# One gather DMA for each sequence by reordered LoRA rows, and the sums of h stored by the sync queue

## The chip, the cores and the metric

The kernel runs on one core of a Trainium2 chip. Its time is what the device takes for one execution, in microseconds (us); lower is better.

## The reference

`x` has 64 sequences of 64 tokens and 512 features, and each sequence has an adapter number from 0 to 7. The first part is a gated MLP with LoRA adapters, the second a matrix of 64x64 for each sequence, chosen by the same number:

```
gate = x @ Wg + (x @ Ag[i]) @ Bg[i]          # 512 -> 2048, rank 16
up   = x @ Wu + (x @ Au[i]) @ Bu[i]
h    = silu(gate) * up
x    = x + h @ Wd + (h @ Ad[i]) @ Bd[i]      # 2048 -> 512
x    = x + einsum('bct,bcd->bdt', x, W1[i])  # mixes the 64 tokens of a sequence
```

## The kernel before

**Tiling.** The first phase (gate, up and h) has 64 steps: 4 groups of 16 sequences (1024 tokens), and in each group 16 chunks of 128 columns of the hidden size. A step makes its chunk of gate and up for a group with seven products of half size in place of eight (a Strassen-like scheme: sums of the quarters of x and of the weights). Every product is made of three matmuls on a high and a low part of each operand (lines 1368 to 1370), for each half of the 256 rows it sums over. The second phase (h times Wd, then the 64x64 mix) goes over 16 blocks of four sequences, again with seven products each (lines 1517 to 1519). It reads h, and the sums and differences of h that its products need, back from `h_dram`.

**The LoRA rows.** The x @ A result of a group is in `t_st`. For each pair of steps (a piece of two chunks, `PIECE = 2`; 32 pieces in all) the tile `bq[n % 2]` holds the rows of B for the 16 sequences of the group, in 4 quads of 4 sequences: for each sequence 16 ranks, and these twice, once for the high and once for the low part of t. That makes 4 sequences x 16 ranks x 2 = 128 partitions. Partition of a row: `half * 64 + sequence * 16 + rank`. Line 1380 multiplies with `bq` and takes 256 columns; its four uses in a step have 4 matmuls each, and the one for `l22_done` comes first, behind the products A11 and S1.

**Gathers.** Which rows of `b_dram` go into `bq` depends on the adapter number, which SP reads into a register (`number`). `gather_b` issues for each sequence two DMAs, one for each half, each of 16 rows of 4 KB (64 KB). A piece takes 32 DMAs, 16 in each of two loop turns of SP. Piece `n` may be issued when piece `n - 2` has been used (`p4_done`), since `bq` has two buffers. The first piece goes another way: `gather_raw` fetches rows of `b_gu` into `bq_raw`, and ACT and POOL split them.

**Queues.** Each engine works in the written order. SP's turn `s` of 1 to 63 loads the weights for step `s + 2` (`load_w`, line 236), stores h of step `s - 1` when it is made (`store_even` or `store_odd`, line 245), gathers half of piece `s // 2 + 1` (line 276), and once in a group loads x of the next (line 241). The sums of h (`hs1` to `hs3`, made by DVE at lines 1001, 1007, 1013 and 1019) are stored by POOL at line 473, whose other work in a step is little: `gather_a` (line 447) copies the A columns of each sequence into `aq`, and a few steps split B for `b_dram`. DVE waits for a store to have landed (`h_stored`) before it writes the same tile again, in `make_s4` even for the store of `hs2` of the step before. Behind the last turn SP issues `load_n4` (line 284), which fills `wd_raw_n4` for the second phase.

Of the kernel before, what the change touches and what calls it, by code (L numbers as in the profile page):

```python
# [11 lines left out]
P = 128  # L12
# [14 lines left out]
PIECE = 2  # L27
PIECES = CH // PIECE
BC = 2 * WB
GATHER = SLOTS * 2 * 16  # L30


PAIRS, KC = 16, CH // 2
# [25 lines left out]
def cond_resid_kernel(nc, x, xg, idx, packed, wd, a_gu, b_gu, a_d, b_d, w1, slot_mask, tok_mask, eye, out):  # L59
    ctx = ExitStack()  # L60
    with ctx:
# [6 lines left out]
        def at(name, offset, shape, dt=F32):  # L68
            return nc.alloc_sbuf_tensor_at(name, shape, dt, offset=base + offset)
# [14 lines left out]
        bq = [at(f"bq{i}", 147456 + i * 16384, [P, QUADS, PIECE, BC], F32R) for i in range(2)]  # L84
        t_st = [[at(f"t_st{u}{i}", 180224 + i * 8192 + u * KIB4, [P, GT], F32R) for i in range(2)] for u in range(2)]
        a_all = at("a_all", 196608, [P, ADAPTERS, KT * 2, RANK])
        aq = [at("aq", 200704, [P, KT * 2, QS, RANK])] + [at(f"aq{q}", 202752 + q * 2048, [P, KT * 2, QS, RANK])
                                                        for q in range(1, QUADS)]
        bq_raw = at("bq_raw", 139264, [P, QUADS, PIECE, WB])
        t_f = at("t_f", 202752, [P, QT])  # L90
# [123 lines left out]
        def piece_of(g, k):  # L214
            return PIECES - 1 - k if g % 2 else k
# [14 lines left out]
        def _(sp):  # L230
# [21 lines left out]
            def store_odd(s):  # L252
# [2 lines left out]
                sp.wait_ge(h1_done, s + 1)  # L255
                store_op(s, H12, h_f[1], 0)

            slot_numbers = {}

            def gather_raw(b):  # L260
                slot_numbers[b] = number(sp, b)
                for half in range(2):
                    r = half * QR + (b % QS) * RANK
                    sp.dma_start(bq_raw[r:r + RANK, b // QS, :, :],
                                 b_gu[0, bass.ds(slot_numbers[b], 1)].rearrange("a r k c -> (a r) k c"))\
                        .then_inc(bq_raw_in[2 * b // SLOTS], 16)

            def gather_b(n, first, last):
                g, k = divmod(n, PIECES)
                sp.wait_ge(b_stored, 16 * (k if g == 0 else PIECES))  # L270
                if n >= 2:
                    sp.wait_ge(p4_done, 2 * n - 2)
                for b in range(first, last):
                    for half in range(2):
                        r = half * QR + (b % QS) * RANK
                        sp.dma_start(bq[n % 2][r:r + RANK, b // QS, :, :].bitcast(F32).rearrange("r k c -> r (k c)"),  # L276
                                     b_dram[piece_of(g, k), bass.ds(slot_numbers[g * SLOTS + b], 1)].rearrange("a r c -> (a r) c"))\
                            .then_inc(bq_in[n % 4], 16)

            def load_parts(op, a, source):  # L280
                k = 0
# [68 lines left out]
            def load_ad(p):  # L350
                if p == 0:
                    sp.wait_ge(p4_done, STEPS - 2)
                else:
                    sp.wait_ge(ad_lo_done, 4 * p)
                for b in range(QS):
                    a = number(sp, seq_of(p, b))
                    sp.dma_start(ad_raw[:, b, :, :, :].rearrange("p e k r -> p (e k r)"),
                                 a_d[bass.ds(a, 1)].rearrange("a p c -> (a p) c")).then_inc(ad_in, 16)
# [24 lines left out]
            for s in range(1, STEPS):  # L383
                if fresh(s + 2):
                    load_w(s + 2)
                if s % 2:
                    store_even(s - 1)
                else:
                    store_odd(s - 1)
                if s >= 2 and s // 2 + 1 < GROUPS * PIECES:  # L390
                    at = s % 2 * (SLOTS // 2)
                    gather_b(s // 2 + 1, at, at + SLOTS // 2)
                if 5 <= s % CH < 13 and s // CH + 1 < GROUPS:
                    for b in range(2 * (s % CH - 5), 2 * (s % CH - 4)):
                        b += (s // CH + 1) * SLOTS
                        slot_numbers[b] = number(sp, b)
                if s % CH == 2 and s // CH + 1 < GROUPS:
                    load_x(s // CH + 1)
                if s == STEPS - CH + 1:
                    load_wd11()  # L400
                    load_wd12()
                if s == STEPS - CH + 2:
                    load_wd22_early()
                if s == STEPS - CH + 3:
                    load_wd21_early()
                if s == STEPS - CH + 7:
                    store_t3()
                if s == STEPS - CH + 11:
                    store_n4()
                if s == STEPS - 2:  # L410
                    load_h(0)
                    load_ad(0)
# [13 lines left out]
            for n in range(3, PAIRS * PRODUCTS):  # L426
                p, i = divmod(n, PRODUCTS)
                if n + 4 < PAIRS * PRODUCTS:
                    load_h(n + 4)
                if i == 3 and p + 1 < PAIRS:  # L430
                    load_bd(p + 1)
                if i == 5 and p + 2 < PAIRS:
                    load_ad(p + 2)
            p = PAIRS - 1
            for j in (1, 0):
                sp.wait_ge(y_done[j], p + 1)
# [4 lines left out]
        def _(pool):  # L441
            def gather_a(g, q):
                if g:
                    pool.wait_ge(t_done, g * QUADS + q)
                for s in range(QS):
                    a = number(pool, g * SLOTS + q * QS + s)
                    pool.tensor_copy(aq[q if g == 0 else 0][:, :, s, :], a_all[:, bass.ds(a, 1), :, :].rearrange("p a k r -> p (a k) r"))\
                        .then_inc(a_gathered, 1)

            def load_b(i):  # L450
# [14 lines left out]
            def bq0_lo(pair):  # L465
# [1 line left out]
                pool.wait_ge(bq0_hi_done, pair + 1)  # L467
                pool.tensor_tensor(bq[0][:, q, :, WB:2 * WB], bq_raw[:, q, :, :], bq[0][:, q, :, 0:WB].bitcast(F32),
                                   ALU.subtract).then_inc(bq0_lo_done, 1)

            def store_sum(s, op, tile, col):
                g, k = s // CH, chunk_of(s) // 2
                pool.dma_start(h_dram[PPG * g:PPG * (g + 1), op, :, k, :].rearrange("q p t -> p q t"),  # L473
                               tile[:, col:col + HALF].rearrange("p (q t) -> p q t", q=PPG)).then_inc(h_stored[op], 16)

            def store_s3(n):
                pool.wait_ge(hs3_done, n + 1)
                store_sum(2 * n, HS3, hs3, 0)

            def store_s12(n):  # L480
                pool.wait_ge(hs1_done, n + 1)
                store_sum(2 * n, HS1, hs1, 0)
                pool.wait_ge(hs2_done, n + 1)
                store_sum(2 * n, HS2, hs2, 0)

            def store_s4(n):
                pool.wait_ge(hs4_done, n + 1)
                store_sum(2 * n, HS4, hs2, 0)

            def load_tables():  # L490
                pool.wait_ge(p4_done, 2 * CH)
# [65 lines left out]
            for s in range(1, STEPS):  # L557
                g, c = divmod(s, CH)
                late = LATE_T if g == 0 else 0
                if s < PIECES:  # L560
                    b_lo(s)
                    store_b(s)
                    if s + 1 < PIECES:
                        load_b(s + 1)
                if g + 1 < GROUPS and 4 <= c - late < 8:
                    gather_a(g + 1, c - late - 4)
                if s == 2 * CH:
                    load_tables()
                if s == 2 * CH + 3:
                    store_tables()  # L570
                if s % 2:
                    store_s3(s // 2)
                    if s >= 3:
                        store_s4(s // 2 - 1)
                else:
                    store_s12(s // 2 - 1)
            load_res(0)
            make_zeros()
            load_mix(0)
            store_s12(STEPS // 2 - 1)  # L580
            load_res(1)
            store_s4(STEPS // 2 - 1)
            for p in range(1, PAIRS):
                load_mix(p)
                if p + 1 < PAIRS:
# [6 lines left out]
        def _(act):  # L592
# [40 lines left out]

            def bq0_hi(pair):
                q = slice(2 * pair, 2 * pair + 2)
                act.wait_ge(bq_raw_in[pair], 16 * SLOTS)
                hi(bq[0][:, q, :, 0:WB], bq_raw[:, q, :, :]).then_inc(bq0_hi_done, 1)

            def t_hi(g, q):
# [721 lines left out]
        def _(pe):  # L1361
# [23 lines left out]
            def lora_a(g, q):  # L1385
                i = g * QUADS + q
                pe.wait_ge(a_gathered, QS * (i + 1))
                if q == 0:
                    for k in range(4):
                        pe.wait_ge(x_in[k], 16 * (g + 1))  # L1390
                bank = T_BANKS[q] if g == 0 else RT
                if g:
                    pe.wait_ge(t_masked, i if q else 1)
                a = aq[q if g == 0 else 0]
                n = slice((q % 2) * QT, (q % 2 + 1) * QT)
                for k in range(KT):
                    src = xst[(B11, B12, B21, B22)[2 * (k // 2) + q // 2]][:, (k % 2) * HALF:(k % 2 + 1) * HALF]
                    m = pe.matmul(bank[:, 0:QT], a[:, k * 2:k * 2 + 2, :, :].rearrange("p u s r -> p (u s r)"),  # L1398
                                  src[:, n], start=k == 0, stop=k == KT - 1)
                m.then_inc(t_done, 1)  # L1400

# [240 lines left out]
```

## Time and profile before

| | |
|---|---|
| median of 3 runs | 1218.6 us (1215.49 to 1220.42) |
| the profiled execution: its time | 1219.65 us |
| its span, first to last instruction | 1218.0 us |
| mean granted TensorE clock | 0.982 of full speed |
| busy: PE, DVE, ACT, POOL | 1163.6, 913.6, 539.3, 256.3 us |
| DMA over the span | 276.26 MB, mean 227 GB/s |

The busy time of PE is modelled from its pipelined matmuls; what it waited for is read from the table of waits. A name like `bq<-b_dram` is a tile and what it was filled from, buffer numbers left out. `SPq` is the sync engine's queue of instructions.

### The profile page before, as it was taken

What the parts mean: (1) busy time and instruction counts of PE and PEld (TensorE: products, weight loads), DVE (VectorE), ACT (ScalarE), POOL (GpSimd) and SP (SyncE); (2) the same over time, 40 slices, a digit from 0 to 9 for tenths busy, and PEclk for the clock granted to TensorE, in tenths of its full rate; (3) what the DMA queues carried; (4) which work ended last, traced back from release to release, by engine and by line L of the source; (5) the groups of instructions that cost most, each with busy time, mean ns of one, the idle gap of its engine ahead of it and who ended that gap; (6) DMA issues with size and microseconds to landing.
All of it is one profiled execution on the core that took longest, in us unless ns stands there. A gap on an engine that the chain in (4) does not pass through costs nothing.

```text
span 1218.0 us, 23035 instructions
## 1 busy us (share of the span) xinstructions
PE 1163.6 (96%) x6720; PEld 1034.8 (85%) x6720; DVE 913.6 (75%) x1578; ACT 539.3 (44%) x902; POOL 256.3 (21%) x405
## 2 busy tenths in 40 slices
PE   4889999999999997999999999998899999999998
PEld 3678888887888886888888788887899999999997
DVE  6776777876787787678887788888667766776775
ACT  4544444543444443344453344456344444444442
POOL 5223221112201012220101111011322221231230
PEclk8899999999999999899999999999999999999999
DMA  5597876688667589666759978868777777667781
GB/s 188 161 308 241 244 222 180 170 235 262 189 180 234 171 238 264 190 194 187 233 166 274 280 223 252 243 215 307 244 265 244 244 239 273 232 230 274 231 277 66
DMA packets 155583, 276.26 MB, mean 227 GB/s; under 512 B 28898, under 2 KB 97634, under 8 KB 155330
## 3 DMA queue, kind: packets, MB, share of 16 engines
q1 hardware_dynamic: 133104, 213.48, 57.5%
q0 software_dynamic: 21488, 59.66, 14.6%
q10 hardware_dynamic: 866, 1.66, 0.4%
q8 instruction: 54, 0.88, 0.3%
q14 instruction: 71, 0.58, 0.2%
HBM read 200.23 MB, written 74.45 MB: 226 GB/s over the span
## 4 chain that ended last, share of the span: by engine, by line
PE 73%; SPq 9%; DVE 5%; DMA 5%; issue 4%; ACT 3%; POOL 1%; POOLq 0%; DVEq 0%; ACTq 0%
PE ps L1368 12%; PE ps L1369 12%; PE ps L1370 12%; PE ps L1517 8%; PE ps L1519 8%; PE ps L1518 8%; PE ps L1380 7%; SPq L276 7%; DMA bq<-b_dram 2%; PE ps L1398 2%; DMA h_raw<-h_dram 1%; DMA xst<-xg 1%; SPq L245 1%; ACT xo_hi L602 1%; SPq L199 1%
## 5 line engine op out<-in xcount | busy, mean ns | idle before, releaser
L1368 PE MATMUL ps<-xo_hi,w_hi 128*128 128x512 f32 x896 | 359.3, 401 | 12.0 <-DVE w_lo L886 10.7
L1369 PE MATMUL ps<-xo_lo,w_hi 128*128 128x512 f32 x896 | 354.8, 396 | 0.0
L1370 PE MATMUL ps<-xo_hi,w_lo 128*128 128x512 f32 x896 | 351.8, 393 | 0.0
L1368 PEld LDWEIGHTS ps<-xo_hi,w_hi 128*128 128x128 f32 x896 | 171.4, 191 | 43.0 <-DVE w_lo L886 10.7
L1370 PEld LDWEIGHTS ps<-xo_hi,w_lo 128*128 128x128 f32 x896 | 170.4, 190 | 38.2
L473 POOL DMA_DIRECT2D h_dram<-hs x128 | 96.0, 754 | 487.3 <-DVE hs L1001 247.9
L886 DVE TENSOR_TENSOR hl<-h_raw,hh 128x1024 fp32r<-128x1024 f32 x112 | 137.0, 1223 | 79.0 <-ACT hh L602 77.6
L1380 PEld LDWEIGHTS ps<-t_st,bq 128*128 128x128 f32 x1024 | 158.5, 193 | 44.2 <-DMA bq<-b_dram 18.0
L1369 PEld LDWEIGHTS ps<-xo_lo,w_hi 128*128 128x128 f32 x896 | 171.1, 191 | 26.6
L1380 PE MATMUL ps<-t_st,bq 128*128 128x256 f32 x1024 | 166.2, 286 | 21.7 <-DMA bq<-b_dram 15.9
L602 ACT ACTIVATE hh<-h_raw 128x1024 fp32r<-128x1024 f32 x112 | 117.9, 1053 | 113.3 <-DMA h_raw<-h_dram 72.0
L886 DVE TENSOR_TENSOR w_lo<-wsum,w_hi 128x512 fp32r<-128x512 f32 x116 | 83.1, 717 | 60.2 <-ACT w_hi L602 60.2
L674 ACT ACTIVATE u_s<-u_s 128x512 f32<-128x512 f32 x64 | 40.5, 633 | 145.6 <-DVE u_s L973 145.6
L1517 PE MATMUL ps<-wd_t,hh 128*128 128x256 f32 x256 | 73.2, 286 | 5.5 <-DVE hl L886 3.8
L1517 PE MATMUL ps<-wd,hh 128*128 128x288 f32 x256 | 76.6, 299 | 0.0
L986 DVE TENSOR_TENSOR h_f<-u_s,v 128x512 f32<-128x512 f32 x64 | 44.2, 690 | 41.7 <-ACT u_s L674 41.7
L1518 PE MATMUL ps<-wd,hh 128*128 128x288 f32 x256 | 75.4, 295 | 0.0
L670 ACT ACTIVATE p_s<-p_s 128x512 f32<-128x512 f32 x64 | 40.5, 633 | 78.5 <-DVE p_s L956 78.4
L1519 PE MATMUL ps<-wd,hl 128*128 128x288 f32 x256 | 75.2, 294 | 0.0
L602 ACT ACTIVATE w_hi<-wsum 128x512 fp32r<-128x512 f32 x116 | 72.2, 623 | 5.4 <-DVE wsum L919 5.4
L1518 PE MATMUL ps<-wd_t,hh 128*128 128x256 f32 x256 | 72.9, 285 | 0.0
L1519 PE MATMUL ps<-wd_t,hl 128*128 128x256 f32 x256 | 72.9, 285 | 0.0
(153 smaller groups left out, 2188.0 us busy)
## 6 DMA issues: line engine op xcount, KB each, us to landing
bq<-b_dram SPq DMA_DIRECT2D x992, 64.0 KB, 2.6
h_raw<-h_dram SPq DMA_DIRECT2D x112, 512.0 KB, 5.3
h_dram<-hs POOLq DMA_DIRECT2D x128, 256.0 KB, 4.2
raw<-packed SPq DMA_DIRECT2D x58, 512.0 KB, 4.0
h_dram<-h_f SPq DMA_DIRECT2D x96, 256.0 KB, 3.9
ad_raw<-a_d SPq DMA_DIRECT2D x64, 128.0 KB, 2.1
xs<-x POOLq DMA_DIRECT2D x16, 512.0 KB, 5.8
y_out_dram<-xs POOLq DMA_DIRECT2D x30, 256.0 KB, 4.7
```

The costliest lines, as they stand in the source:

```text
L276: sp.dma_start(bq[n % 2][r:r + RANK, b // QS, :, :].bitcast(F32).rearrange("r k c -> r (k c)"), b_dram[piece_of(g, k), bass.ds(slot_number ...
L473: pool.dma_start(h_dram[PPG * g:PPG * (g + 1), op, :, k, :].rearrange("q p t -> p q t"), tile[:, col:col + HALF].rearrange("p (q t) -> p q ...
L602: return act.activation(dst, src, ACT.Copy)
L886: return dve.tensor_tensor(dst, src, hi.bitcast(F32), ALU.subtract)
L986: dve.tensor_tensor(h_f[s % 2][:, HALF:GT], u2_s[:, :], v22[:, :], ALU.mult).then_inc(h2_done, 1)
L1368: pe.matmul(bank, st[0], mv[0], start=start and kk == 0, stop=False, skip_group_check=True)
L1369: pe.matmul(bank, st[0], mv[1], start=False, stop=False, skip_group_check=True)
L1370: m = pe.matmul(bank, st[1], mv[0], start=False, stop=kk == 1, skip_group_check=True)
L1380: m = pe.matmul(bank[:, i * QT:(i + 1) * QT], b[:, q, c % PIECE, a:a + P], t_st[u][g % 2][:, q * QT:(q + 1) * QT], start=start and part == ...
L1517: pe.matmul(bank[:, 0:width], h_hi, w[:, 0:width], start=start and k == 0, stop=False, skip_group_check=True)
L1518: pe.matmul(bank[:, 0:width], h_hi, w[:, width:2 * width], start=False, stop=False, skip_group_check=True)
L1519: return pe.matmul(bank[:, 0:width], h_lo, w[:, 0:width], start=False, stop=False, skip_group_check=True)
```

## The change

Three edits go together. The rows of `bq` and `bq_raw` are laid out anew: partition `(half * 16 + rank) * 4 + sequence`, so the 32 rows of one sequence stand 4 partitions apart. `aq` (the weights of the matmul that makes t) and `slot_mask` follow that order. Since both halves of a sequence now have one step between their rows, one DMA fills all 32; its source is the 16 rows of `b_dram` with a leading dimension of 2 and step 0 (`to_broadcast`). And the four stores of the sums move from POOL's queue to SP's, at the end of its turn; the last ones (n == 8 and n == 11) stand in SP's loop of the second phase.

```diff
-GATHER = SLOTS * 2 * 16
+GATHER = SLOTS * 16
...
-        aq = [at("aq", 200704, [P, KT * 2, QS, RANK])] + ...
+        aq = [at("aq", 200704, [P, KT * 2, RANK, QS])] + ...
...
+            def store_s3(n):
+                sp.wait_ge(hs3_done, n + 1)
+                store_op(2 * n, HS3, hs3, 0)
+            def store_s12(n):
+                sp.wait_ge(hs1_done, n + 1)
+                store_op(2 * n, HS1, hs1, 0)
+                sp.wait_ge(hs2_done, n + 1)
+                store_op(2 * n, HS2, hs2, 0)
+            def store_s4(n):
+                sp.wait_ge(hs4_done, n + 1)
+                store_op(2 * n, HS4, hs2, 0)
...
             def gather_raw(b):
                 slot_numbers[b] = number(sp, b)
-                for half in range(2):
-                    r = half * QR + (b % QS) * RANK
-                    sp.dma_start(bq_raw[r:r + RANK, b // QS, :, :],
-                                 b_gu[0, bass.ds(slot_numbers[b], 1)].rearrange("a r k c -> (a r) k c"))\
-                        .then_inc(bq_raw_in[2 * b // SLOTS], 16)
+                sp.dma_start(bq_raw[b % QS:P:QS, b // QS, :, :].rearrange("r k c -> r (k c)"),
+                             b_gu[0, bass.ds(slot_numbers[b], 1)].rearrange("a r k c -> a r (k c)").to_broadcast([2, RANK, PIECE * WB]))\
+                    .then_inc(bq_raw_in[2 * b // SLOTS], 16)
...
                 for b in range(first, last):
-                    for half in range(2):
-                        r = half * QR + (b % QS) * RANK
-                        sp.dma_start(bq[n % 2][r:r + RANK, b // QS, :, :].bitcast(F32).rearrange("r k c -> r (k c)"),
-                                     b_dram[piece_of(g, k), bass.ds(slot_numbers[g * SLOTS + b], 1)].rearrange("a r c -> (a r) c"))\
-                            .then_inc(bq_in[n % 4], 16)
+                    sp.dma_start(bq[n % 2][b % QS:P:QS, b // QS, :, :].bitcast(F32).rearrange("r k c -> r (k c)"),
+                                 b_dram[piece_of(g, k), bass.ds(slot_numbers[g * SLOTS + b], 1)].to_broadcast([2, RANK, PIECE * BC]))\
+                        .then_inc(bq_in[n % 4], 16)
...
                     gather_b(s // 2 + 1, at, at + SLOTS // 2)
+                if s % 2:
+                    store_s3(s // 2)
+                    if s >= 3:
+                        store_s4(s // 2 - 1)
+                else:
+                    store_s12(s // 2 - 1)
...
+                if n == 8:
+                    store_s12(STEPS // 2 - 1)
+                if n == 11:
+                    store_s4(STEPS // 2 - 1)
...
-                    pool.tensor_copy(aq[q if g == 0 else 0][:, :, s, :], ...)
+                    pool.tensor_copy(aq[q if g == 0 else 0][:, :, :, s], ...)
...
-            (store_sum, store_s3, store_s12, store_s4 and their calls in gpsimd)
...
-                act.wait_ge(bq_raw_in[pair], 16 * SLOTS)
+                act.wait_ge(bq_raw_in[pair], 16 * SLOTS // 2)
...
-                    m = pe.matmul(bank[:, 0:QT], a[:, k * 2:k * 2 + 2, :, :].rearrange("p u s r -> p (u s r)"),
+                    m = pe.matmul(bank[:, 0:QT], a[:, k * 2:k * 2 + 2, :, :].rearrange("p u r s -> p (u r s)"),
...
-        "slot_mask": (np.arange(P)[:, None] % QR // RANK == np.arange(QS)[None, :]).astype(np.float32),
+        "slot_mask": (np.arange(P)[:, None] % QS == np.arange(QS)[None, :]).astype(np.float32),
```

## Rows read from the trace of the kernel before

**Rows 1.** Busy time by stretch: engines (x instructions), PEclk, DMA share, GB/s.

```profile
60.00:110.00 50.00, 45.40 (x219) 38.02 (x218) 34.87 (x58) 21.24 (x35) 13.60 (x17) 0.97 0.85 272
110.00:822.00 712.00, 699.46 (x3477) 591.80 (x3476) 561.81 (x934) 314.27 (x502) 121.74 (x180) 0.99 0.75 220
```

**Rows 2.** Waits of PE: us in total, times, longest.

```profile
PE ps L1380 <- DMA bq<-b_dram: 15.9, 5, 7.2
...
PE ps L1380 <- POOL bq L468: 5.9, 2, 3.7
PE ps L1398 <- POOL aq L447: 4.9, 1, 4.9
```

**Rows 3.** The chain that ended last, 420 to 830: start, us, what.

```profile
480.08 1.27 SPq L276
481.45 6.13 DMA bq<-b_dram
487.62 1.22 PE ps L1380 x4
...
812.49 7.19 DMA wd_raw_n<-wd_dram
```

**Rows 4.** SP in order of time: start, us, line, DMAs.

```profile
3.73 24.88 SPq L264 DMA_DIRECT2D bq_raw<-b_gu  x32
...
29.27 15.86 SPq L276 DMA_DIRECT2D bq<-b_dram  x32
```

**Rows 5.** SP in order of time, one turn's gathers, within 260 to 300.

```profile
273.77 8.50 SPq L276 DMA_DIRECT2D bq<-b_dram  x16
```

**Rows 6.** DMA issues over the span: KB each, us from issue to landing.

```profile
bq<-b_dram SPq DMA_DIRECT2D x992, 64.0 KB, 2.6
...
xst<-xg ACTq DMA_DIRECT2D x2, 512.0 KB, 8.5
...
a_all<-a_gu ACTq DMA_DIRECT2D x1, 512.0 KB, 12.3
...
eye_f<-eye ACTq DMA_DIRECT2D x1, 64.0 KB, 12.7
idx_i<-idx ACTq DMA_DIRECT2D x1, 0.2 KB
smask<-slot_mask ACTq DMA_DIRECT2D x1, 2.0 KB, 12.4
tmask<-tok_mask ACTq DMA_DIRECT2D x1, 16.0 KB, 12.0
```

**Rows 7.** DMA queues over the span: packets, MB, share of 16 engines (q10 is ACT's).

```profile
q1 hardware_dynamic: 133104, 213.48, 57.5%
...
q10 hardware_dynamic: 866, 1.66, 0.4%
```

**Rows 8.** The queues in 5 to 12 us.

```profile
q1 hardware_dynamic: 348, 1.27, 45.1%
```

**Rows 9.** The queues in 424 to 430 us.

```profile
q1 hardware_dynamic: 352, 0.72, 45.9%
```

**Rows 10.** All DMA in 110 to 822 us, and its gathers.

```profile
DMA packets 101619, 156.98 MB, mean 220 GB/s; under 512 B 19250, under 2 KB 70915, under 8 KB 101420
...
bq<-b_dram SPq DMA_DIRECT2D x899, 64.0 KB, 2.6
```

**Rows 11.** PE in order of time: first LoRA matmuls of steps 4 and 62.

```profile
90.94 1.22 PE L1380 MATMUL ps<-t_st,bq 128*128 128x256 f32 x4 [4.20 <-DMA bq<-b_dram]
...
801.75 0.64 PE L1380 MATMUL ps<-t_st,bq 128*128 128x256 f32 x4
```

**Rows 12.** DVE in order of time, the last sum before `load_n4`.

```profile
812.60 0.69 DVE L1019 TENSOR_TENSOR hs<-h_f,hs 128x512 f32<-128x512 f32 x1
```

**Rows 13.** Groups of instructions on POOL: busy us, mean ns, idle before.

```profile
L473 POOL DMA_DIRECT2D h_dram<-hs x128 | 96.0, 754 | 487.3 <-DVE hs L1001 247.9 <-DVE hs L1007 223.2 <-DVE hs L1019 13.2
...
L447 POOL COPY aq<-a_all 128x128 f32 x64 | 36.1, 582 | 98.0 <-PE ps L1398 85.6 <-issue 12.0
```

More of the change, by code:

```diff
@@ L86, in cond_resid_kernel @@
         a_all = at("a_all", 196608, [P, ADAPTERS, KT * 2, RANK])
-        aq = [at("aq", 200704, [P, KT * 2, QS, RANK])] + [at(f"aq{q}", 202752 + q * 2048, [P, KT * 2, QS, RANK])
+        aq = [at("aq", 200704, [P, KT * 2, RANK, QS])] + [at(f"aq{q}", 202752 + q * 2048, [P, KT * 2, RANK, QS])
                                                         for q in range(1, QUADS)]
@@ L446, in gather_a @@
                     a = number(pool, g * SLOTS + q * QS + s)
-                    pool.tensor_copy(aq[q if g == 0 else 0][:, :, s, :], a_all[:, bass.ds(a, 1), :, :].rearrange("p a k r -> p (a k) r"))\
+                    pool.tensor_copy(aq[q if g == 0 else 0][:, :, :, s], a_all[:, bass.ds(a, 1), :, :].rearrange("p a k r -> p (a k) r"))\
                         .then_inc(a_gathered, 1)
@@ L469, in bq0_lo @@
                                    ALU.subtract).then_inc(bq0_lo_done, 1)
[L471 to L488, printed above, removed]
             def load_tables():
@@ L570, in _ @@
                     store_tables()
[L571 to L576, printed above, removed]
             load_res(0)
@@ L579, in _ @@
             load_mix(0)
-            store_s12(STEPS // 2 - 1)
             load_res(1)
-            store_s4(STEPS // 2 - 1)
             for p in range(1, PAIRS):
```

## The prediction

> **What bounds the kernel now.** I read the busy times and the table by stretches first. From 110 to 822 us, nearly the whole first phase, PE is busy for 699.5 of 712 us [rows 1]. So PE sets the pace, and what is idle elsewhere costs nothing. Next, the waits of PE: the gathers are its largest one, 15.9 us in five pieces, and POOL's split of the first piece costs it 5.9 [rows 2]. The chain shows what such a wait hangs on: the last gather DMA of a piece is issued at 480 us, needs 6.1 us to land, and only then do the matmuls of line 1380 run [rows 3]. SP in order of time shows why it is late. A turn's 16 gathers take it 8.5 us, or 0.53 us each [rows 5], out of a step of 12.3 us ((801.75 - 90.94) / 58 steps [rows 11]). The DMA engines are busy for 85% of 60 to 110 us and 75% of the rest of the phase [rows 1], with room of about a quarter when all 16 share the load. Fewer and larger gathers can win back at most the 15.9 us, plus some of the 5.9. They can lose far more if they change how the bytes are spread over the DMA engines, so that is the question I put most work into.
>
> **The gathers, part by part.** Removed: 496 of 992 issues at line 276 and 16 of 32 at line 264. A turn of SP then spends about 4.2 us less (8 x 0.53 [rows 5]). The raw gathers of 24.9 us [rows 4] halve to 12.4. The bytes stay: 992 x 64 KB [rows 6] is 65 MB, now in 496 DMAs of 128 KB.
>
> How is one DMA spread? Rows bear on it in one place, ACT's queue. ACT issues seven DMAs [rows 6]: two of x and `a_all`, each 128 rows of 4 KB, `eye`, `smask` and `tmask` with one packet for each of 128 rows, and the index load of a single row. That makes 6 x 128 + 1 = 769 packets with data. The queue shows 866 [rows 7]. The 97 others are 6 x 16 + 1: sixteen completions, one for each engine, for each DMA of 128 rows, and one for that of one row. So the number of engines follows from the outermost dimension of the access pattern. All gathers of before have 16 rows outermost on both sides, hence 16 engines. The new gather's destination has 32 rows, but its source has an outermost dimension of 2 (step 0), which can't be merged with the 16 rows under it. A split that must cut both sides evenly at the outermost dimension has 2 parts: two engines, 16 rows of 4 KB each. I forecast this; the trace shows the ends 1 and 16 of it, not a 2. Nor does a row show whether it would be the same two each time. I assume so; if the pair moved on from gather to gather, the load would be even and the first rival's time would come out, and its chance holds this too.
>
> The Trainium skill has this as a rule ("DMA: Bandwidth & Descriptors", section "Why a DMA increments its semaphore by 16 and not by 1", and again under "Rules for kernel authors"): the number of engines is the largest one up to 16 that divides the slowest dimension of both patterns, the lowest-numbered engines are used, and a leading zero-stride broadcast of c copies confines the DMA to at most c engines. By that rule the sum is the one of 2085 us below; by the sixteen that every gather of before has it is the 1205 us of the first rival. The one-row load agrees with the rule.
>
> Price of two engines. One piece puts 16 x 64 KB = 1.05 MB on each of them. The rate of one engine: 1.27 MB at 45.1% of 16 engines x 7 us is 25.1 GB/s [rows 8]; over the whole span q1 has 213.48 MB in 57.5% of 16 x 1218 us, 19.1 GB/s [rows 7]; in a stretch of gathers alone 0.72 MB in 45.9% of 16 x 6 us, 16.3 GB/s [rows 9]. That gives 41.8, 55.0 or 64.3 us for a piece. I take the fast end: the slow rows have 16 engines writing to 16 neighbouring partitions at once, and two engines won't crowd each other. To that comes the engine's sixteenth of all else: 156.98 MB less 899 x 64 KB (58.9 MB) is 98.1 MB in 712 us [rows 10], 211 KB for each engine in the 24.5 us of a piece, 11.1 us at 19.1 GB/s. A piece thus occupies those two engines for 52.9 us, against the 24.5 us in which PE uses one up. There are two buffers and SP issues half a piece each turn, so the two engines always have a queue, and PE waits at each even step.
>
> Sum: the first gathers of this kind start at 29 us [rows 4] (the raw ones, 32 KB on each of two engines, 16 x 1.3 us, keep them busy until about then); 31 pieces x 52.9 = 1640 us; from the first LoRA matmul of step 62, which needs the last piece, to the end are 1218.0 - 801.75 = 416 us [rows 11]. Together 2085 us of span. The profiled execution had 1.65 us around its span and lies 1.05 us above the median, so the two nearly cancel: 2085. Bounds: everything at 25.1 GB/s gives 50.2 for a piece and 2001; all at 19.1 gives 66.1 and 2494; gathers at 16.3 give 75.4 and 2782. A PE that idles half the time may also be granted the lower clock, 1.2 for 2.4 GHz. A step would then take up to 25 us; two of them still fit in 52.9, and only the last two steps would add some 24.
>
> **The sums of h.** POOL loses 128 issues of 0.75 us [rows 13], SP gains 128 of about 0.5 (62 us in all, less than the 260 that the gathers give back). POOL had 487 us idle before them, so its relief is worth nothing. On SP they stand behind the turn's gathers, which cover the time until DVE has made the sum. Behind them waits the next `load_w`, with a step in hand: nothing. Twice it is not hidden. `load_n4` is on the chain (issued at 812.49, lands 7.2 us later [rows 3]) and now stands behind `store_s3` and `store_s4` of the last turn; DVE ends that sum at 813.3 [rows 12], and one more issue follows, so it is 1.3 to 2 us later: +2. And `make_s4` waits for the store of `hs2` of the turn before. With two slow engines an eighth of that store queues behind half a piece, so DVE, and PE with it, waits there too; this is the same queue, already counted.
>
> **The layout.** `aq` is written with a step of 4 elements. The copy takes 582 ns with a dense output [rows 13]; none with a step is in the trace. Between nothing and twice as long: POOL is idle most of the time, and PE waited for it 4.9 us at the start [rows 2], where 16 copies would add up to 9 us. I take nothing, since the input already has short runs, and keep 9 for the range. Matmuls read the same count of rows and columns: nothing.
>
> **The rivals.**
> - *All 16 engines share the gathers, and the stalls go.* Speaks for it: every gather of before ran so. Against: none had an outermost 2. Then 15.9 us go and 2 come: 1218.6 - 13.9 = 1205, between 1199 (with the 5.9 too) and 1214. It decides from 8 engines up: (2.10 MB / k) at 25.1 GB/s plus 11.1 us fits in 24.5 us for k above 6.3. Chance 0.11.
> - *16 engines, nothing gained.* The five stalls would be those of a busy DMA (85% [rows 1], 6.1 us to land against 2.6 as a median [rows 3, 6]) and not of SP's issuing; the bytes are the same. 1213 to 1224. Chance 0.04.
> - *16 engines, a little slower.* `make_s4` waits for `hs2` stored late from SP, or the copies to `aq` cost their 9 us. 1225 to 1235. Chance 0.02.
> - *Four engines.* If dimensions were balanced some other way: 20.9 + 11.1 = 32 us a piece, 992 + 445 = 1437. Chance 0.02.
>
> **How the numbers follow.** Two engines get 0.81. Within it 1850 to 2550 takes in both rates of the bounds that I think possible and holds nearly all of it (0.78 of the whole); it is the likeliest case's own range, and I keep to it, since the gap from 1240 to 1850 is nearly empty. A measurement here tells about 0.5% from no change. Faster 0.11; within 0.5% 0.04; slower 0.81 + 0.02 + 0.02 = 0.85.
>
> **What would show it.** Two engines: in the first phase the DMA share of the 16 falls to between a fifth and a half while the gathers take 20 us or more to land; PE waits 25 to 30 us for `bq<-b_dram` at every even step, some 800 us in all; ACT's and POOL's own busy times hardly move. SP's issues of line 276 grow long if the two queues fill up. If I am wrong, a gather lands in about 3 us, SP's turn has 8 gathers in about 4 us, the 15.9 us of waits shrink, and the span is near 1205. The forecast falls at one step, that a source with an outermost 2 is cut in two; the size falls if an engine alone runs much faster or slower than 25 GB/s.

## The result, and the profile after

| | before | after |
|---|---|---|
| median | 1218.66 us | 1982.97 us (1980.32 to 1984.67, 4 runs) |
| ratio | | 1.627 (95%: 1.624 to 1.631) |
| span of the profiled execution | 1218.0 us | 1978.6 us |
| granted TensorE clock | 0.982 | 0.822 |

The forecast was 2085 us, in a range of 1850 to 2550, with 0.85 for slower. The waits of PE answer to [rows 2] (us in total, times, longest):

```profile
PE ps L1373 <- DMA bq<-b_dram: 397.0, 31, 20.5
PE ps L1361 <- DVE v L956: 249.1, 30, 14.7
...
PE ps L1373 <- POOL bq L488: 5.9, 2, 3.8
PE ps L1391 <- POOL aq L467: 4.9, 1, 4.9
```

Line 1373 is line 1380 of before. All 31 gathered pieces are late, where 5 were. The second wait is new, 249 us for DVE. DVE waits for the stores of the sums to land before it writes their tiles again; that this is the same delay by another way is shown by the run `pool_sums` below.

```profile
DVE hs L1006 <- DMA h_dram<-hs: 405.0, 30, 18.9
DVE hs L1012 <- DMA h_dram<-hs: 319.1, 31, 17.2
```

Where the time goes is seen in single stretches (busy us of PE, PEld, DVE, ACT, POOL, then PEclk, DMA share, GB/s):

```profile
606.00:610.00 4.00, 0.00 (x0) 0.00 (x0) 3.91 (x8) 1.46 (x3) 0.00 (x0) 0.55 0.13 52
625.00:629.00 4.00, 1.01 (x4) 1.01 (x5) 0.00 (x0) 0.00 (x0) 0.00 (x0) 0.50 0.92 262
```

From 606 to 610 us the DMA share is 0.13 of 16 engines, which is 2 of 16, and they move 52 GB/s, 26 for each. PE does nothing and is granted about half its clock (0.55), near the 1.2 GHz level. At 625 us a burst comes through at 262 GB/s with 0.92 of the engines busy; I read it as the load of weights that SP issued from 616 us on. From 600 to 700 us the rate goes to and fro between plateaus of 52 GB/s and such bursts. SP's queue at that time answers to [rows 5]:

```profile
612.00 2.81 SPq L245 DMA_DIRECT2D h_dram<-hs  x2
616.31 8.37 SPq L236 DMA_DIRECT2D raw<-packed  x1
624.73 0.98 SPq L245 DMA_DIRECT2D h_dram<-h_f  x2
625.97 10.50 SPq L286 DMA_DIRECT2D bq<-b_dram  x8
636.52 7.08 SPq L245 DMA_DIRECT2D h_dram<-hs  x2
645.04 3.23 SPq L236 DMA_DIRECT2D raw<-packed  x1
648.32 0.64 SPq L245 DMA_DIRECT2D h_dram<-h_f  x1
649.21 10.24 SPq L286 DMA_DIRECT2D bq<-b_dram  x8
659.50 8.01 SPq L245 DMA_DIRECT2D h_dram<-hs  x2
```

Two turns of SP, one piece, take 47.5 us (612.00 to 659.50). Eight gathers take 10.5 us where sixteen took 8.5 before, and one load of weights holds SP for 8.37 us where it took 0.37. The trace names no wait inside an issue; my reading is that an issue also waits for room behind earlier DMAs. It would explain why the chain that ended last now names SP for 67% of the span: it points at the engine that was blocked, not at the cause.

The packet counts settle the number of engines. The row of q1, before in [rows 7]:

```profile
q1 hardware_dynamic: 185328, 246.98, 37.1%
```

It has 52,224 packets more. The 128 stores of the sums that moved to this queue bring 128 x (512 + 16) = 67,584 (256 KB in pieces of 512 bytes, and 16 completions). So 15,360 went elsewhere: the data rows are the same, 1024 gathers lost 16 completions each, 16,384, and 512 gathers brought 1,024, two each. Two runs below confirm both parts. In `sums_sp`, where only the stores moved, q1 has 200,688 packets, exactly 67,584 more than before. In `pool_sums`, where the stores stay with POOL, it has 117,744, exactly 15,360 fewer.

### The profile page after: what moved, and what is told of

Same layout as the page of the kernel before. It is cut to its first block, busy times and chain, and to the rows that moved or that the text cites. A ratio compares the mean times of both kernels' runs of the same rounds, so it can differ in the third digit from the quotient of the medians.

```text
span 1978.6 us, 22011 instructions
## 1 busy us (share of the span) xinstructions
PE 1293.4 (65%) x6720; PEld 1125.9 (57%) x6720; DVE 909.4 (46%) x1578; ACT 538.3 (27%) x902; POOL 161.9 (8%) x277
## 4 chain that ended last, share of the span: by engine, by line
SPq 67%; PE 17%; DMA 7%; issue 6%; DVE 3%; ACT 1%; DVEq 0%; ACTq 0%
SPq L286 28%; SPq L245 24%; SPq L236 9%; PE ps L1510 4%; PE ps L1512 4%; PE ps L1511 4%; DMA bq<-b_dram 3%; DMA h_dram<-hs 2%; SPq L199 2%; DMA h_raw<-h_dram 2%; SPq L241 1%; PE ps L1361 1%; PE ps L1362 1%; PE ps L1363 1%; PE ps L1373 1%
## 5 line engine op out<-in xcount | busy, mean ns | idle before, releaser
L1361 PE MATMUL ps<-xo_hi,w_hi 128*128 128x512 f32 x896 | 401.6, 448 | 261.0 <-DVE v L956 249.1
L1373 PE MATMUL ps<-t_st,bq 128*128 128x256 f32 x1024 | 192.8, 318 | 402.9 <-DMA bq<-b_dram 397.0
L1362 PE MATMUL ps<-xo_lo,w_hi 128*128 128x512 f32 x896 | 389.9, 435 | 0.0
L1363 PE MATMUL ps<-xo_hi,w_lo 128*128 128x512 f32 x896 | 383.4, 428 | 0.0
L1361 PEld LDWEIGHTS ps<-xo_hi,w_hi 128*128 128x128 f32 x896 | 195.3, 218 | 302.4 <-DVE v L956 255.6
L1362 PEld LDWEIGHTS ps<-xo_lo,w_hi 128*128 128x128 f32 x896 | 194.5, 217 | 32.3
L1006 DVE TENSOR_TENSOR hs<-hs,h_f 128x512 f32<-128x512 f32 x32 | 22.1, 692 | 405.1 <-DMA h_dram<-hs 405.0
L1012 DVE TENSOR_TENSOR hs<-h_f,hs 128x512 f32<-128x512 f32 x32 | 22.1, 692 | 319.1 <-DMA h_dram<-hs 319.1
L659 ACT ACTIVATE u_s<-ps 128x512 f32<-128x512 f32 x64 | 38.3, 598 | 479.4 <-PE ps L1363 479.4
L467 POOL COPY aq<-a_all 128x128 f32 x64 | 38.1, 666 | 472.6 <-PE ps L1391 465.9
```

Of the source, the lines that this page charges most:

```text
L1361: pe.matmul(bank, st[0], mv[0], start=start and kk == 0, stop=False, skip_group_check=True)
L1362: pe.matmul(bank, st[0], mv[1], start=False, stop=False, skip_group_check=True)
L1363: m = pe.matmul(bank, st[1], mv[0], start=False, stop=kk == 1, skip_group_check=True)
L1373: m = pe.matmul(bank[:, i * QT:(i + 1) * QT], b[:, q, c % PIECE, a:a + P], t_st[u][g % 2][:, q * QT:(q + 1) * QT], start=start and part == ...
```

## The experiments

Twelve kernels ran, each beside the kernel before on the same chip.

**Two gathers again (`two_dma`).** The new row order and the stores on SP stay. The edit is shown against the changed kernel.

```diff
-  sp.dma_start(bq[n % 2][b % QS:P:QS, ...], b_dram[...].to_broadcast([2, RANK, PIECE * BC]))
+  for half in range(2):
+      r = half * QR + b % QS
+      sp.dma_start(bq[n % 2][r:half * QR + QR:QS, ...], b_dram[...].rearrange("a r c -> (a r) c"))
```

> The new row order and the sums of h on SP stay, but each sequence is fetched by two DMAs of 16 rows again (992 + 32 gathers, 16 rows outermost on both sides). If the outermost 2 of the source is the cause: all 16 engines again, PE waits for bq under 30 us, 1205 to 1240 us (SP issues 18 DMAs a turn, the same 16 gathers and two stores more than before, about 10 us of a step of 12.3). If the step of 4 partitions or the stores on SP were the cause: it stays above 1500 us.

Measured: 1378.8 us, ratio 1.133 (1.128 to 1.137). The 604 us to the changed kernel are the leading 2's. But 161 us against the kernel before stay, and neither of my two ranges (1205 to 1240, above 1500) holds the measured time: PE waits 74.8 us for `bq`, not under 30. This is followed up below.

**Two copies of B, adjacent (`near`) and apart (`apart`).** POOL writes each piece of B twice, so that one DMA reads 32 rows without a step of 0. Adjacent copies make 32 rows outermost; copies far apart make 2.

```diff
# near: b_dram (PIECES, ADAPTERS, 2, RANK, ...)
+  b_dram[piece, bass.ds(slot, 1)].rearrange("a e r c -> (a e r) c")
# apart: b_dram (2, PIECES, ADAPTERS, RANK, ...)
+  b_dram[:, piece, bass.ds(slot, 1)].rearrange("e a r c -> e (a r) c")
```

> As the changed kernel, but POOL writes each piece of B twice into b_dram, one copy behind the other for each adapter, so that the source of a gather is 32 rows in a row with no step of 0; one DMA a sequence of 128 KB. The raw gathers of the first piece are two DMAs each. If the outermost dimension decides: 32 on both sides, 16 engines, 496 x 16 completions, 1195 to 1215 us. If it were the larger DMA or the rows 4 partitions apart: above 1500 us.

> The same two copies of B, but the second one far away in b_dram, so that the source of a gather has an outermost dimension of 2 with a true step in place of 0, and no row is read twice by one DMA. If the outermost 2 decides: as the changed kernel, 1950 to 2010 us, and 2 completions for each of 496 gathers (q1 has 14880 - 512 packets fewer in gathers than 992 + 32 gathers of 16 completions would give). If the step of 0 (reading rows twice) were the cause: 1195 to 1225 us.

Measured: near 1233.9 us, ratio 1.015 (1.010 to 1.020), above my range of 1195 to 1215 and far below 1500; apart 1992.1 us, ratio 1.637, within its range. The rows of q1, first near:

```profile
q1 hardware_dynamic: 192752, 247.01, 63.7%
```

and apart:

```profile
q1 hardware_dynamic: 185808, 246.98, 37.1%
```

The run with two gathers has 200,688 packets there. Near has 7,936 fewer, 496 x 16: one set of 16 completions for each sequence. Apart has 14,880 fewer, which leaves 496 x 2. Both kernels write as much and gather the same bytes; neither has a step of 0. So the outermost dimension of 2 is the cause, shown, and reading a row twice is not.

**One of the two ways for every other sequence (`half`).** As `two_dma`, but sequences of even number are fetched by one DMA with the leading 2.

> As the run with two gathers a sequence and the stores on SP, but every other sequence is fetched by one DMA with the leading 2. On the two engines a piece then puts 8 x 64 KB (20.2 us at 26 GB/s) + 8 x 8 KB (2.5) + about 7 us of other data = 30 us. If the load on two engines decides: 30 us for a piece, against 31 us that SP's turns take in the run with two gathers and less here (12 issues for 16), so 1340 to 1400 us. If the whole loss came from each such DMA by itself (its own latency), half of the 605 us between the two runs: about 1680 us.

Measured: 1448.0 us, ratio 1.191, above the range that I gave and far below 1680. SP issues 12 gathers a turn here. `near_half`, below, has the same eight leading 2's in a piece with 8 issues a turn and takes 1457.5. The two also differ in where the sums are stored and in how often B is written, and near_half is 16 us behind by the end of step 8, up to which B is written (its last LoRA matmul starts at 199.4 us, here at 183.6). From there to the end of the phase, 27.5 pieces, near_half takes 31.2 us a piece and half 31.3. Four issues fewer a turn gain nothing, so what bounds both is the load on the two engines.

**Stores back on POOL (`pool_sums`).** The leading 2 stays.

> The changed kernel with the stores of the sums back on POOL's queue. If the load on two engines sets the time, the bytes on them are the same: 1930 to 2000 us, though DVE's waits for these stores shrink or move to PE's wait for bq. If the stores' place on SP behind the gathers sets it (DVE waited 724 us for them): below 1800 us.

Measured: 1977.3 us, ratio 1.624, within the first range. The two waits of PE become one:

```profile
PE ps L1376 <- DMA bq<-b_dram: 702.8, 31, 31.1
```

397 + 249 us before are 703 now, and the time is the same. The stall at DVE was where the two engines' delay came out, not a cost of its own.

**How much load on two engines (`near_quarter`, `near_half`).** Adjacent copies, stores with POOL (`near_pool`, below, is their base), but 4 or 8 of the 16 gathers of a piece read the first copy through a leading 2; SP issues 16 gathers a piece in all.

```diff
+  rows = rows[:, 0].to_broadcast([2, RANK, PIECE * BC]) if b % 4 < 1 else rows.rearrange("a e r c -> (a e r) c")
```

> Two adjacent copies of B, sums with POOL, 16 gathers a piece, but 4 of them read the first copy twice through a leading 2. The two engines get 4 x 64 KB + 12 x 8 KB + about 180 KB of the rest = 0.54 MB a piece, 21 us at 26 GB/s, below the 24.5 us in which PE uses a piece up. If their load decides by a threshold: 1235 to 1255 us, as without them (1240). If each such DMA costs in proportion: 1240 + a quarter of 737 = 1424.

> The same with 8 of 16 gathers through a leading 2: 8 x 64 + 8 x 8 + 180 KB = 0.77 MB for each of the two engines, 29.6 us a piece, above 24.5. By the load on the two engines 31 x 5.1 = 158 us more than 1240, less the stalls already in it: 1360 to 1410 us. In proportion: 1608.

Measured: 1265.6 and 1457.5 us, against 1239.9 with none and 1977.3 with all 16 (`pool_sums`). The last LoRA matmul of the first phase starts at (none, a quarter, half, all):

```profile
L1379 PE MATMUL ps<-t_st,bq x1024: 274/283/582, 41.6 to 839.5; 128*128 128x256 f32 x171
```

```profile
L1380 PE MATMUL ps<-t_st,bq x1024: 274/283/583, 40.9 to 864.3; 128*128 128x256 f32 x171
```

```profile
L1380 PE MATMUL ps<-t_st,bq x1024: 274/283/583, 41.0 to 1057.5; 128*128 128x256 f32 x171
```

```profile
L1376 PE MATMUL ps<-t_st,bq x1024: 274/283/583, 39.6 to 1576.1; 128*128 128x256 f32 x171
```

The first four gathers cost 25 us, the next four 193, the last eight 519. The last eight are (1576.1 - 1057.5) / 31 pieces = 16.7 us a piece, 2.1 us each. Proportion is ruled out.

Taken from the end of step 8 on, where B has been written, a piece lasts 23.9, 24.9, 31.2 and 48.1 us. An estimate of the load on each of the two engines, with 211 KB of other data as in the prediction and 26 GB/s, is 13.2, 22.0, 30.8 and 48.5 us. So the load does not matter while it is below the pace of PE, and sets the time above it; between 8 and 16 gathers I measured no point. Both medians lie above what I had expected (by 11 us at the quarter, 47 at the half). At the half, 18 us are lost by the end of step 8 (199.4 us against 181.6 in near_pool), and I had counted 180 KB of other data, not 211. At the quarter the load comes close to PE's pace, and it costs 1 us a piece; that it is uneven within a piece would explain this, but I did not test it.

**One half of the rest each: the row order (`layout`), the stores (`sums_sp`).** Both start from the kernel before, with two gathers a sequence.

> The kernel before with the new row order alone: two DMAs of 16 rows for each sequence, rows 4 partitions apart; the sums of h stay with POOL. In the run with two gathers and the stores on SP an issue took 0.67 us against 0.53 before, so 16 of them cost SP 2.2 us more a turn: 8.1 to 8.5 become 10.7, the turn about 12.3, just what a step takes. If the rows' spacing is what makes an issue longer: 0.67 us again and 1220 to 1280 us. If it was the traffic of the stores: 0.53 us and 1213 to 1223.

> The kernel before with the sums' stores moved to SP alone, old row order, 16-row gathers. My prediction priced the move at +2 us. If SP's turn is what it costs (8.5 gathers, 1.1 for two stores, 1 to 2 us of waiting for DVE's sums, 1.4 for the rest: 12.5 to 13 us against 12.3 of a step): 1225 to 1290 us. If hidden as predicted: 1216 to 1224.

Measured: layout 1321.0 us, ratio 1.087 (1.081 to 1.093), above both of my ranges; sums_sp 1245.1, ratio 1.023 (1.018 to 1.027), within the first of its two. SP issues of the gathers, layout (ns min/median/max):

```profile
L276 SPq DMA_DIRECT2D bq<-b_dram x992: 495/536/3218, 34.6 to 894.0; - x199
```

and the kernel before:

```profile
L276 SPq DMA_DIRECT2D bq<-b_dram x992: 315/367/3064, 29.3 to 797.5; - x199
```

The stores are POOL's in both. Rows 4 partitions apart make the same DMA of 16 rows 0.17 us longer to issue. What that does to SP's turn in layout, line by line:

```profile
409.82 10.96 SPq L276 DMA_DIRECT2D bq<-b_dram  x16
422.33 0.36 SPq L236 DMA_DIRECT2D raw<-packed  x1
422.74 0.99 SPq L245 DMA_DIRECT2D h_dram<-h_f  x2
423.99 11.13 SPq L276 DMA_DIRECT2D bq<-b_dram  x16
436.36 0.35 SPq L236 DMA_DIRECT2D raw<-packed  x1
```

A turn is 14.0 us (422.33 to 436.36), of which 11.1 are gathers. I had expected 12.3, which is what a step had, so SP now sets the pace. In sums_sp the gathers take 8.3 us as before, and two sums add 1:

```profile
404.64 0.96 SPq L245 DMA_DIRECT2D h_dram<-hs  x2
407.55 0.36 SPq L236 DMA_DIRECT2D raw<-packed  x1
408.63 8.27 SPq L290 DMA_DIRECT2D bq<-b_dram  x16
416.94 0.97 SPq L245 DMA_DIRECT2D h_dram<-hs  x2
417.95 1.42 SPq L245 DMA_DIRECT2D h_dram<-h_f  x2
419.64 8.16 SPq L290 DMA_DIRECT2D bq<-b_dram  x16
```

Hardly a gap is left, but for 1.9 us between the sums and the next load (405.60 to 407.55), for which the trace names no wait. From step 8 to the end of the phase a step takes 12.6 us on average, against 12.25 in the kernel before. Alone the parts cost about 105 and 30 us, together 161 (`two_dma`). The 128 stores take SP about 62 us in all. On top of the row order they cost 56, nearly in full, since SP sets the pace there; by themselves half of that. With 8 gathers a turn (`near`) neither shows like this.

**Adjacent copies with the stores on POOL (`near_pool`).**

> One DMA of 32 rows a sequence from two adjacent copies of B, sums of h with POOL. If the 20 us that the run with the stores on SP lost in the first 8 steps came from the sums' stores behind the gathers: they vanish and 1205 to 1218 us remain. If they came from writing B twice (a store of a piece lands in 7.9 us and gathers wait for it): 1220 to 1235 us.

Measured: 1239.9 us, ratio 1.020 (1.016 to 1.024), so not better than near, and 5 us above the higher of my two ranges. The last LoRA matmuls of step 8 start at 147.87 us in the kernel before and at 181.29 here:

```profile
181.29 0.64 PE L1379 MATMUL ps<-t_st,bq 128*128 128x256 f32 x4
```

So 33 us are lost by then, and at the end of the phase only 839.5 - 822.1 = 17.4. After step 8 single gathers win back 16 us. The loss is that of the start, where B is written, and the stores of the sums on SP are not its cause: near, which has them there, is only 20 us behind at step 8 (167.99). After step 8, though, near takes 4 us more than near_pool. The stores of B have 8 adapters outermost on one side and 128 partitions on the other. In near they land in 8.8 us, in apart, with 128 rows on both sides, in 4.8 (medians of 16 each). Each store in near also brings 128 more packets to POOL's queue (14,448 in all against 12,400). Why they land later, and whether that is a matter of fewer engines, I did not separate.

**A start as before, single gathers after it (`hybrid`, `hybrid_sp`).** Group 0 is the kernel before. POOL copies B from HBM to a second tensor, twice, during steps 9 to 23; groups 1 to 3 take the new row order and single DMAs of 32 adjacent rows. `slot_mask` holds both orders. In `hybrid_sp` the sums are stored by SP besides.

```diff
+  if g:
+      sp.wait_ge(b_copied[piece_of(g, k) // 2], 32)
+      for b in range(first, last):
+          sp.dma_start(bq[n % 2][b % QS:P:QS, ...], b_two[piece, bass.ds(slot, 1)].rearrange("a e r c -> (a e r) c"))
+      return
...
+  pool.dma_start(b_two[2 * pair:2 * pair + 2, :, e].rearrange("p a r c -> (p a) (r c)"),
+                 b_dram[2 * pair:2 * pair + 2].rearrange("p a r c -> (p a) (r c)")).then_inc(b_copied[pair], 16)
```

> The kernel before in its first group (two DMAs of 16 adjacent rows, old row order). POOL copies B twice into a second tensor in the background of steps 9 to 23 (8 DMAs of 1 MB, HBM to HBM), and groups 1 to 3 use the new row order and one DMA of 32 adjacent source rows for each sequence. Sums of h stay with POOL. The run with two copies from the start won back 16 us after step 8 and lost 33 before it. If both carry over: 15 us less than before, plus up to 6 for the copies' traffic: 1203 to 1211 us. If the lost time was not the start but the layout: 1215 to 1235.

> As the other hybrid, with the sums' stores on SP as in the change. With 8 gathers of about 0.63 us a turn (5 us) SP has 5 us of room in a step, so the stores should be hidden from group 1 on, and in group 0 they cost about 1 us (the run with only the stores moved was 0.9 behind at the end of group 0). load_n4 stands behind them: +2. 1204 to 1214 us, 0 to 5 above the other hybrid. If the order on SP costs by itself and not by SP's lack of time: 1225 or more.

Measured: hybrid 1207.0 us against 1214.3, ratio 0.994 (0.992 to 0.997), within its range and the only version faster than the kernel before, by 0.6%. The gathers' wait [rows 2] fell from 15.9 to 3.9 us for `b_dram`, which only group 0 reads, and 0.4 for the second tensor:

```profile
PE ps L1399 <- DMA bq<-b_dram: 3.9, 3, 2.2
```

The last LoRA matmuls of step 15, the end of group 0, start at 235.71 us, 1.2 before those of the kernel before, and those of step 63 16.6 us before: groups 1 to 3 win back 15.4. The traced spans differ by as much (1202.6 against 1218.0), but they are the fastest execution of hybrid and a slower one of the kernel before; the medians differ by 7.2.

hybrid_sp took 1225.6 us, ratio 1.009 (1.007 to 1.011), above the 1204 to 1214 that I expected, where I had put a cost of the order on SP by itself. It is 18.9 us behind hybrid in the traces, of which 12.9 come before group 1, where 16 gathers and the sums share SP's turn and the copies of B run:

```profile
183.06 0.36 SPq L238 DMA_DIRECT2D raw<-packed  x1
183.46 0.43 SPq L247 DMA_DIRECT2D h_dram<-h_f  x1
184.14 11.66 SPq L299 DMA_DIRECT2D bq<-b_dram  x16
195.85 0.97 SPq L247 DMA_DIRECT2D h_dram<-hs  x2
198.90 0.36 SPq L238 DMA_DIRECT2D raw<-packed  x1
199.30 4.70 SPq L247 DMA_DIRECT2D h_dram<-h_f  x2
```

That turn takes 15.8 us. By the last LoRA matmuls of step 15 it is 11.7 us behind the kernel before (248.60 against 236.90), and at the end of the phase 0.8 ahead. Neither part alone does this: at the same point hybrid, with the same copies, is 1.2 us ahead of the kernel before, and sums_sp, with the same stores, 0.9 behind (237.82). Only together do they cost 12 us there. The gathers' turn of 11.66 us, against 8.3, fits SP having no room left for issues that get longer; the remaining 3 us in groups 1 to 3 and 3 in the second phase I did not follow up.

## Why the prediction was right

**What bounds it: right.** PE set the pace before, and the split of a gather over DMA engines was the question that mattered.

**Two engines, and always the same two: right, shown.** 2 completions for each gather, a DMA share of 0.13, and the pair of runs `apart` and `near`. At 52 GB/s a gather of 128 KB takes 2.5 us, and SP issues one every 1.3 us from 601.57 us on, so several are under way at 606 to 610 us; yet the share stays at 0.13. The Trainium skill's rule ("DMA: Bandwidth & Descriptors", section "Why a DMA increments its semaphore by 16 and not by 1"), the largest number up to 16 that divides the slowest dimension of both sides, held at 2 and 32 with a step of 0 and without one, and at 32 and 32. Rotating pairs, which would have kept the load even, are ruled out by the plateaus at 52 GB/s and by the time; which two engines they are no row shows.

**The price of a piece: somewhat high.** I had 52.9 us. Each engine moves 26 GB/s, not 25.1. If the other data went at that rate as well, and not at the 19.1 that I took from the whole span: (1.049 + 0.211) MB / 26 GB/s = 48.5 us, which fits. Measured: 47.5 over SP's two turns; from the first such gather's issue at 33.2 us to the last piece's matmuls at 1559.1, 49.2 for each of 31, the loads of x and Wd included. The first LoRA matmuls of step 62 come at 1559 us, where I had 1669:

```profile
1559.10 1.22 PE L1373 MATMUL ps<-t_st,bq 128*128 128x256 f32 x4 [11.77 <-DMA bq<-b_dram]
```

The rest, 1978.6 - 1559.1 = 419.5 us, is the 416 that I took plus little. The sum was 5% high for that one term. The choice of the fast rate was right, but my reason for it was not: I said that the slower rows have 16 engines writing to 16 neighbouring partitions, yet the fast row [rows 8] lies within SP's raw gathers [rows 4], which do the same. And with the rows 4 partitions apart (`layout`) q1 is busy for 53.4% of 1319.3 us, 704 us, against 700 before, for the same 213.48 MB. Why the rate is 26 here and 19 before no run shows, so there is luck in this term: at 19.1 GB/s it would have given 2494 us.

**What would show it: right in kind, the wait smaller.** The DMA share was to fall to between a fifth and a half, and it is 0.34. SP's gathers did grow long. How long one takes to land the profile does not give. I forecast a wait of PE of 25 to 30 us at each even step, 800 in all. Measured are 397 there and 249 at DVE, 646 together or 21 for a piece. With the stores on POOL it is 703, up to 31 us at a time. I had seen DVE's wait coming as part of the same queue, and it was. The wait is smaller for two reasons: a piece is 3.7 us shorter than I took it, and PE itself is slower (row as in [rows 1]):

```profile
110.00:1590.00 1480.00, 854.56 (x3630) 705.59 (x3631) 586.19 (x977) 330.05 (x526) 41.86 (x68) 0.78 0.34 114
```

Its granted clock is 0.78 in this phase against 0.99 before, and its busy time over the span rose from 1163.6 to 1293.4 us. Since the load of the two engines by itself accounts for the 48 us of a piece, these 130 us lie within it: they shorten the wait and add nothing to the total. The 24 us that I held possible for the last two steps at the lower clock did not come either, since the 419.5 us hold only 3.5 more than I took.

**The first rival's price was wrong, though it didn't decide.** I put 1205 us on a gather spread over all engines. The change's own layout and stores don't allow that with two gathers (1379), and one spread gather costs a second copy of B (1234 to 1240, about where I had put the third rival, for another reason). Two terms failed. For the row order I priced the matmuls and the copy to `aq`, but not SP's issue, which takes 0.17 us more each. For the sums' stores I took 2 us, having set their 62 us against the 260 that the gathers would give back; alone they cost 30. The stall part was right in kind: in hybrid the 15.9 us are down to 4.3, and the median falls by 7.2.

**`load_n4` later by 1.3 to 2 us: right.** In sums_sp it is issued 1.8 us after the last h store of the phase (831.96 to 833.78 us), in the kernel before 0.5 (811.99 to 812.49, where [rows 3] show its transfer).

## What to carry to other kernels

Before merging two DMAs by a broadcast, look at what stands outermost in both access patterns, since here it decided over how many engines the bytes went. Count completions per DMA in the queue's packets to see it, and look for plateaus of the DMA share at a small fraction. A DMA share far below one is no proof of room: two engines were full while the mean was a third. And when a sequencer's turn nearly fills a step, price every issue in it, its form included.

## What the runs showed of the hardware that I had not expected

- An issue by SP of 16 rows takes 0.367 us with adjacent partitions and 0.536 with rows 4 partitions apart (medians of 992). For 32 such rows from 32 adjacent source rows it takes 0.472 (medians of 496 and 384), less than for 16.
- Two DMA engines alone move 52 GB/s of 4 KB rows, 26 each.
- The spacing of the destination partitions changed how long an issue takes, but not how long q1 was busy (700 us in before, 704 in layout).
- With two engines full, SP was held up in issuing DMAs, also such as use all 16: a weight load took it 8.37 us, and a gather up to 6.2 us.
